# Four stacks of a rounded part and a rest in layers 0 and 1: put together by transfers instead of matrix products

## The reference

```python
# a0: causal windows of 128, 16 heads of 8 features
scores = einsum('bhqd,bhkd->bhqk', wq, wk) * scale
attn = softmax(where(mask, neg, scores));  outs.append(einsum('bhqk,bhkd->bhqd', attn, wv))
# a1: linear attention, 16 heads of 8 features, 64 random features each
q = (x @ Wq).reshape(b, l, 16, 8);  k, v = ...
qf = relu(q @ Wf + bf);  kf = relu(k @ Wf + bf)
kv = einsum('blhf,blhd->bhfd', kf, v)
out = einsum('blhf,bhfd->blhd', qf, kv) / maximum(qf . kf.sum(1), 1e-6)
return out.reshape(b, l, d) @ Wo + bo
```

## Time and profile before

| | us |
|---|---|
| median of 3 runs | 1827.08 (1820.6 to 1829.6) |
| profiled execution, its own time | 1828.14 |
| its span in the trace | 1826.3 |
| PE busy (matrix products) | 1547.0, 85% of the span |
| DVE busy | 1240.9, 68% |
| ACT busy | 1001.1, 55% |
| POOL busy | 792.5, 43% |

### The profile page before, as it was taken

The page is one execution under the profiler, slowest core; times in us unless marked ns, Lnnn a source line. Parts: engine busy times, 40 slices in busy tenths (PEclk is TensorE's granted clock), DMA queues, the critical chain, the costliest instruction groups (busy, mean ns, idle before and its releaser), DMA issues.

```text
span 1826.3 us, 28809 instructions
## 1 busy us (share of the span) xinstructions
PE 1547.0 (85%) x10698; PEld 843.6 (46%) x10748; DVE 1240.9 (68%) x2857; ACT 1001.1 (55%) x1927; POOL 792.5 (43%) x734
## 2 busy tenths in 40 slices
PE   7789889877988898977798888997679898999867
PEld 4555564313555566432355555542135554655214
DVE  5555648998564465799865455499976445559996
ACT  4465436665556443766555544566545654455754
POOL 2231215786133212679614131178941412118892
PEclk9899999978999998988799999999879999989979
DMA  6014302020201430212110152031111015202110
GB/s 234 35 35 129 101 6 76 30 93 17 77 1 35 135 94 7 76 41 81 47 46 1 36 162 73 7 93 45 55 47 41 1 41 167 63 6 93 48 52 12
DMA packets 78028, 111.31 MB, mean 61 GB/s; under 512 B 6208, under 2 KB 56384, under 8 KB 77632
## 3 DMA queue, kind: packets, MB, share of 16 engines
q1 hardware_dynamic: 75840, 105.28, 18.5%
q0 software_dynamic: 2048, 4.20, 0.7%
HBM read 93.73 MB, written 15.73 MB: 60 GB/s over the span
## 4 chain that ended last, share of the span: by engine, by line
PE 47%; DVE 24%; ACT 11%; issue 8%; POOL 6%; DMA 3%; SPq 2%; DVEq 0%; POOLq 0%; ACTq 0%
PE P L241 10%; DVE M L2071 9%; PE P L1685 4%; POOL M L2141 3%; PE P L1914 3%; PE P L409 2%; PE P L2199 2%; PE P L223 2%; DVE st L188 1%; PE P L1861 1%; DVE M L203 1%; PE P L397 1%; ACT P L2006 1%; PE P L981 1%; DVE M L1782 1%
## 5 line engine op out<-in xcount | busy, mean ns | idle before, releaser
L2071 DVE TENSOR_TENSOR_SCAN M<-P,M 128x512 f32<-128x512 f32 x384 | 442.6, 1200 | 22.5 <-ACT P L2006 21.9
L2006 ACT ACTIVATE P<-M,negA 128x512 f32<-128x512 f32 x384 | 262.8, 689 | 175.9 <-DVE M L2071 171.8
L241 PEld LDWEIGHTS P<-wt,M 128*128 128x128 f32 x2176 | 278.8, 196 | 104.6 <-issue 38.7
L241 PE MATMUL P<-wt,M 128*128 128x128 f32 x2176 | 298.0, 284 | 17.5 <-DVE M L1782 6.4
L1914 PE MATMUL P<-M,wt 32*32 32x512 f32 x3072 | 236.0, 689 | 85.2 <-DVE M L2071 62.0
L2141 POOL TENSOR_TENSOR M<-M 128x512 f32<-128x512 f32 x192 | 238.2, 1276 | 96.0 <-ACT M L1988 77.2
L2141 POOL TENSOR_TENSOR M<-W,M 128x512 f32<-128x512 f32 x192 | 244.3, 1306 | 40.9 <-PE P L1914 40.4
L1914 PEld LDWEIGHTS P<-M,wt 32*32 32x32 f32 x3072 | 39.7, 110 | 230.3 <-DVE M L2071 152.9
L1685 PE MATMUL P<-M,wt 128*128 128x512 f32 x256 | 135.8, 612 | 8.0 <-ACT M L1743 4.7
L1782 DVE TENSOR_TENSOR M<-M,P 128x512 f32<-128x512 f32 x128 | 85.8, 675 | 65.5 <-PE P L1693 47.9
L1734 ACT ACTIVATE M<-P 128x512 f32<-128x512 f32 x128 | 75.9, 593 | 90.4 <-PE P L1685 90.1
(11 more groups left out here) (359 smaller groups left out, 3019.9 us busy)
## 6 DMA issues: line engine op xcount, KB each, us to landing
M<-in_e SPq DMA_DIRECT2D x112, 192.0 KB, 2.5
W<-in_e SPq DMA_DIRECT2D x8, 1536.0 KB, 8.0
M<-dt SPq DMA_DIRECT2D x48, 256.0 KB, 4.6
W<-du SPq DMA_DIRECT2D x32, 256.0 KB, 4.9
M<-in_e SPq DMA_DIRECT2D x8, 960.0 KB, 5.3
M<-in_e SPq DMA_DIRECT2D x8, 576.0 KB, 6.4
M<-xs SPq DMA_DIRECT2D x16, 256.0 KB, 3.0
ys<-M SPq DMA_DIRECT2D x16, 256.0 KB, 2.3
```

Of the source, the lines that this page charges most:

```text
L241: m = e.matmul(out[:, tok(j)], h[:, tok(j)], wgt, start=first and j == 0, stop=last, skip_group_check=True)
L2006: e.activation(t["aa"][n % 2][:, :], t["dtr"][i][:, :], EXP, scale=negA[:, c:c + 1]).then_inc(ACT.s, ACT.mark(b, "a3", "aa", n))
L2071: e.tensor_tensor_scan(bb[:, :], t["aa"][n % 2][:, :], bb[:, :], 0.0, MUL, ADD).then_inc(DVE.s, DVE.mark(b, "a3", "scan", n))
```

## The change

1. The selection matrix `sst`, PE's 192 products with it (32 + 32 + 64 + 64) and ACT's 96 copies are gone.
2. A helper `stack_parts` issues three transfers per stack, each of 32 rows by 512 values (64 KB), from the on-chip tiles `hi`, `lo` and `hi` into the stack. All are issued by SP: 12 per item in a0, 24 in a1, 288 in all. Each stack has a semaphore of its own, and PE waits for 48 on it.
3. In a0 the steps stand in `sp_attn0` behind `fetch_firsts`; a1 has a new SP function `sp_attn1`. In a1 stacks of keys and of queries share four tiles (`stk`): the transfer of query stack `g` waits for the key product `kf 2g+1`, the last that reads key stack `g`.
4. In a1 the query projection moves to the front, beside those of keys and values (L903 of the changed kernel; L991 before, after `kv 5`), and the rest of the queries gets a tile of its own.
5. The masks of rows in `by_query` and `by_key` are cut to the 96 and 112 rows that count.
6. All five tables of turns are new.

```diff
+        def stack_parts(e, dst, hi, lo, g, done):
+            r = slice(32 * g, 32 * g + 32)
+            for i, src in enumerate((hi, lo, hi)):
+                e.dma_start(dst.bitcast(f32)[32 * i:32 * i + 32, :], src.bitcast(f32)[r, :]).then_inc(done, 16)
...
         def pe_attn0(e, w, b):
-            def stack_q(g):
-                e.matmul(P[2 + g % 2][:, :], sst[:, tok(g)], qhi[:, :], start=True, stop=False, skip_group_check=True)
-                e.matmul(P[2 + g % 2][0:96, :], sst[:, 128 * g + 32:128 * g + 128], qlo[:, :], start=False,
-                         stop=True, skip_group_check=True).then_inc(PE.s, PE.mark(b, "a0", "stk", g))
...
-                w.wait_ge(DVE.s, DVE.of(b, "a0", "qlo" if g == 0 else "v"))
-                stack_q(g)
             for n, (a, gs) in enumerate(A0_QUERY):
-                if n in (1, 2):
-                    yield
-                    w.wait_ge(ACT.s, ACT.of(b, "a0", "qst", n - 1))
-                    stack_q(n + 1)
                 yield
-                w.wait_ge(ACT.s, ACT.of(b, "a0", "qst", gs[-1]))
+                for g in gs:
+                    w.wait_ge(a0_qst_in[b % 2][g], 48 * (b // 2 + 1))
...
         def act_attn0(e, w, b):
-            for g in range(4):
-                yield
-                w.wait_ge(PE.s, PE.of(b, "a0", "stk", g))
-                e.activation(qst[g][:, :], P[2 + g % 2][:, :], COPY).then_inc(ACT.s, ACT.mark(b, "a0", "qst", g))
...
         def pe_attn1(e, w, b):
-            def stack(hi, g, i, name):
-                a1_bank_free(w, b, i)
-                out = a1_bank(L, i)[0:96, :]
-                e.matmul(out, sst[:, 128 * g:128 * g + 96], hi[:, :], start=True, stop=False)
-                e.matmul(out, sst[:, 128 * g + 32:128 * g + 128], lo[:, :], start=False, stop=True).then_inc(
-                    PE.s, PE.mark(b, "a1", name, g))
             def features(u):
-                w.wait_ge(ACT.s, ACT.of(b, "a1", "kst", g))
+                w.wait_ge(a1_kst_in[b % 2][g], 48 * (b // 2 + 1))
             def qfeat(c):
-                w.wait_ge(ACT.s, ACT.of(b, "a1", "qst", g))
+                w.wait_ge(a1_qst_in[b % 2][g], 48 * (b // 2 + 1))
...
+            e.matmul(a1_bank(L, A1_Q)[:, :], wv("a1q"), xn[:, :], start=True, stop=True).then_inc(
+                PE.s, PE.mark(b, "a1", "q"))
...
         def act_attn1(e, w, b):
-            def copy_stack(dst, g, i, name):
-                w.wait_ge(PE.s, PE.of(b, "a1", name, g))
-                e.activation(dst[0:96, :], a1_bank(L, i)[0:96, :], COPY).then_inc(ACT.s, ACT.mark(b, "a1", name, g))
...
+        def sp_attn1(e, w, b):
+            L, s = lanes[b % 2], b % 2
+            khi, stk, klo, qhi, qlo = L.R[10], L.R[11:15], L.R[15], L.R[16], L.R[6]
+            yield
+            w.wait_ge(POOL.s, POOL.of(b, "a1", "ones"))
+            w.wait_ge(ACT.s, ACT.of(b, "a1", "khi"))
+            w.wait_ge(DVE.s, DVE.of(b, "a1", "klo"))
+            for g in range(4):
+                stack_parts(e, stk[g], khi, klo, g, a1_kst_in[s][g])
+            for g in range(4):
+                yield
+                if g == 0:
+                    w.wait_ge(ACT.s, ACT.of(b, "a1", "qhi"))
+                    w.wait_ge(DVE.s, DVE.of(b, "a1", "qlo"))
+                w.wait_ge(PE.s, PE.of(b, "a1", "kf", 2 * g + 1))
+                stack_parts(e, stk[g], qhi, qlo, g, a1_qst_in[s][g])
...
         def sp_attn0(e, w, b):
             fetch_firsts(e, b, lanes[b % 2].W[:, :], 0, 8)
+            L, va, negm, kst, qst, pT = a0_tiles(b)
+            yield
+            w.wait_ge(ACT.s, ACT.of(b, "a0", "qhi"))
+            w.wait_ge(DVE.s, DVE.of(b, "a0", "qlo"))
+            for g in range(4):
+                stack_parts(e, qst[g], L.R[11], L.R[12], g, a0_qst_in[b % 2][g])
             if 3 <= b + 1 < NB:
...
         TURNS = {
-            "tensor": (2131,
+            "tensor": (2027,
```

More of the change, by code:

```diff
@@ L443, in pe_attn0 @@
                 if n in (6, 7):
-                    w.wait_ge(ACT.s, ACT.of(b, "a0", "qst", n - 4))
+                    w.wait_ge(DVE.s, DVE.of(b, "a0", "v"))
                 elif n > 1:
@@ L899, in a1_bank_free @@
             last = A1_USES[i - 2]
-            if last in ("klo", "qlo"):
-                w.wait_ge(DVE.s, DVE.of(b, "a1", last))
+            if i < 4:
+                w.wait_ge(DVE.s, DVE.of(b, "a1", *last))
             else:
@@ L954, in pe_attn1 @@
             m.then_inc(PE.s, PE.mark(b, "a1", "v"))
-            yield
-            w.wait_ge(DVE.s, DVE.of(b, "a1", "klo"))
-            stack(khi, 0, A1_S[0], "kst")
-            yield
-            stack(khi, 1, A1_S[1], "kst")
+            e.matmul(a1_bank(L, A1_Q)[:, :], wv("a1q"), xn[:, :], start=True, stop=True).then_inc(
+                PE.s, PE.mark(b, "a1", "q"))
             yield
@@ L987, in pe_attn1 @@
                     yield from turn_kv(0)
-                if u == 5:
-                    yield
-                    a1_bank_free(w, b, A1_Q)
-                    e.matmul(a1_bank(L, A1_Q)[:, :], wv("a1q"), xn[:, :], start=True, stop=True).then_inc(
-                        PE.s, PE.mark(b, "a1", "q"))
-                if u >= 6:
-                    yield
-                    w.wait_ge(DVE.s, DVE.of(b, "a1", "qlo"))
-                    stack(qhi, u - 6, A1_QS[u - 6], "qst")
             yield from qfeat(0)
@@ L1104, in dve_attn1 @@
             kvm = L.M[:, 17 * T:17 * T + 256].rearrange("p (c n) -> p c n", c=8)
-            khi, lo, qhi = R[10], R[15], R[16]
+            khi, klo, qhi, qlo = R[10], R[15], R[16], R[6]
             if b == 0:
@@ L1110, in dve_attn1 @@
             w.wait_ge(ACT.s, ACT.of(b, "a1", "khi"))
[L1111 to L1112 removed]
+            e.scalar_tensor_tensor(klo[:, :], a1_bank(L, A1_K)[:, :], 1.0, khi.bitcast(f32), MUL, SUB).then_inc(
                 DVE.s, DVE.mark(b, "a1", "klo"))
             yield
+            w.wait_ge(ACT.s, ACT.of(b, "a1", "qhi"))
+            e.scalar_tensor_tensor(qlo[:, :], a1_bank(L, A1_Q)[:, :], 1.0, qhi.bitcast(f32), MUL, SUB).then_inc(
+                DVE.s, DVE.mark(b, "a1", "qlo"))
+            yield
+            w.wait_ge(POOL.s, POOL.of(b, "a1", "ones"))
             w.wait_ge(PE.s, PE.of(b, "a1", "v"))
@@ L1126, in keys_by_values @@
                                 over_tokens(wv("kvmask")), MUL).then_inc(DVE.s, DVE.mark(b, "a1", "kvm", h))
-            for u in range(8):
-                if u == 5:
-                    yield
-                    w.wait_ge(ACT.s, ACT.of(b, "a1", "qhi"))
-                    w.wait_ge(PE.s, PE.of(b, "a1", "kst", 3))
-                    e.scalar_tensor_tensor(lo[:, :], a1_bank(L, A1_Q)[:, :], 1.0, qhi.bitcast(f32), MUL, SUB).then_inc(
-                        DVE.s, DVE.mark(b, "a1", "qlo"))
-                if u == 4:
-                    yield from keys_by_values(0)
+            yield from keys_by_values(0)
             yield from keys_by_values(1)
```

140 lines of the change are left out of this document (40 added, 100 removed).

## The result

The changed kernel takes 1894.45 us (median of 4 runs, 1885.41 to 1898.59), against 1827.51 for the kernel before in the same session (4 runs, 1820.6 to 1829.6). The ratio is 1.0377, with a 95% interval of 1.0342 to 1.0413. It is slower, by 67 us; I had said 1827, and 1803 to 1846 as the range.

A forecast was written before the change was run, and what follows sets the result against it. The prediction took the touched stages as close to bound by PE, with 10 to 15% idle. From 1828.14 us, +26.5 for the start, −34 for stacks and +6 for waits gave 1826.6, said as 1827, range 1803 to 1846.

The forecast's parts named there:

- Start, +26.5: First pair's a0: first stack lands at 48.0 us behind all first loads, costing 26.5 us with the clock loss.
- three us at half speed: Behind the long wait at the start: the clock falls to 1.2 GHz for three us, losing 1.5 us.
- Stacks, −34: a0 and a1: removing PE's stack products and ACT's copies gains 34 us, between 30.5 and 49.
- What is on the path: Chain from 99.38 to 1512.98 us: stack products 25.1 us and ACT's copies 5.4, together 30.5 us as the gain's lower end.
- my sum: Whole kernel: start, stacks and waits add to 1826.6 us, said as 1827, own range 1817 to 1837; chance 40%.
- Waits, +6: Entries to a0 and a1 behind the start: four of 14 waits for stacks left uncovered at 1.5 us, 6 us.
- the slower rival: a0 and a1 entries: uncovered waits of 17 to 21 us take the gain, 1841 us; chance 23%.
- 0 for the rest: All else, such as DVE, POOL, cut rows, ACT's relief beyond the 5.4 us counted, SP in f1: no effect.
- SP in f1: f1: six stack issues by SP delay the sorted tokens, at most 2 us per pair, 8 in all, 1835 us; chance 6%.
- the cases: Whole kernel: the sum 1827 us (40%), waits 1841 (23%), PE bound 1806 (24%), start not lost 1819 (7%), SP 1835 (6%).

The follow-up runs named there:

- a_start: The changed kernel with the first stacks' transfers issued between the loads of the weights, not behind all loads; 1865.71 us, 1.0234.
- c_old_start: The changed kernel with the turns of the kernel before, and the first stacks' transfers between the loads of the weights; 1875.78 us, 1.0268.
- i_none: The changed kernel in the turns of before, with neither stack transfers nor stack products; readers of a stack read the rounded part; 1850.26 us, 1.0145.
- e_both: c_old_start with the removed stack products issued again beside the transfers, read by nobody; 1861.12 us, 1.0201.
- p_prod: i_none with the removed stack products issued again, read by nobody, and no transfers; 1836.36 us, 1.0070.
- n_new_none: a_start (new turns) with neither stack transfers nor stack products; readers of a stack read the rounded part; 1838.67 us, 1.0069.
- m_new_both: a_start (new turns) with the removed stack products issued again beside the transfers, read by nobody; 1867.31 us, 1.0223.
- k_a1q: The kernel before with transfers for a1's query stacks alone, and the early query projection; 1835.93 us, 1.0067.

## Why the prediction was wrong

**The account.** Span = PE's work at full clock + what the lower clock adds (half of the time at it) + PE's idle time. That half is an upper bound, since PE is idle in part of that time and since products took 1.4 to 1.6 times as long in the rows above, not twice. It is also what the Trainium skill gives as the penalty (TensorE: Matmul & The Clock Gate, "Terms"). From each profile's span, busy time and mean clock, in us:

| kernel | work | clock | idle | span |
|---|---|---|---|---|
| before | 1421 | 126 | 279 | 1826.3 |
| a_start | 1361 | 179 | 325 | 1864.5 |
| c_old_start | 1365 | 184 | 327 | 1875.6 |
| i_none | 1368 | 163 | 317 | 1847.3 |
| e_both | 1417 | 139 | 301 | 1856.7 |
| p_prod | 1424 | 130 | 280 | 1834.0 |

In a_start the change takes 60 us of work away, adds 53 by the clock and 46 of idle time: +38. The differences between the rows are what counts here, not their heights.

**Start, +26.5: right as a sum, with a piece too small.** The wait of 28.03 us, the landing and the row were as said, and a_start measures 24 to 29. But I had three us at half speed, for a loss of 1.5, and it was nearly 12. The first pair ends 35 us late in all, and part of that is not the place in SP's row: a_start still has 16.5 of it.

**Stacks, −34: the step that failed.** The work did go: 0.5 us a stack gave 48, and the account has 56 (1421 to 1365). What failed is "What is on the path": I took each piece on the chain as time that its removal returns. Its removal cost 14 us instead (p_prod to i_none; 15 from e_both to c_old_start). In the score phase DVE sets the pace, and PE's stack products stood in waits that are there anyway. Taking them away made the waits longer, and at 0.50 clock the products left took over the time. c_old_start, e_both, i_none and p_prod show it in the turns of before. In the new turns n_new_none, with neither products nor transfers, is 14 us over the kernel before where my sum had a gain. But m_new_both, with the products back, gains nothing, so the way by waits and clock is there carried over and not shown. I had the earlier trace rows with a wait of 3.53 us and the clock at 0.50 behind it, and priced that once, at the start, with 1.5 us; the same price could fall due wherever the change opens a wait. With neither products nor transfers the kernel was to be 30 to 49 us faster by my sum, and is 24 slower (14 in the new turns). p_prod has PE's products in place and no transfers, and stands 11 us over before. That belongs to what else the new form has, perhaps the early projection (k_a1q has it too, and stands at +12); no run parts them.

**Waits, +6: mis-sized.** The transfers cost 25 to 29 us beside the place in SP's row. In the traces a part of that lies in the first pair (8 of 28 from i_none to c_old_start, 18 of 33 from n_new_none to a_start), and 15 to 20 behind it, against the 6 of my sum. PE's waits ended by a transfer came to 17 us behind the start in the changed kernel, as in the slower rival, for issues of 0.6 to 0.7 us instead of 0.33 and an entry of 4.2 instead of 3.1. Such waits are again no price by themselves: they are 28.6 us in c_old_start, which has only 11 us more idle time than i_none but 21 more by the clock.

**"0 for the rest"**: the new turns were worth −7 to −10, if that is told from chance, SP in f1 about 1 us in the pair read; no run has ACT's relief alone. The range failed as all the cases rested on the stacks' removal being a gain; none had PE's remaining work get slower behind the start.

By terms, each by its distance from the kernel before in its own session, the 67 us are 24 for the start (a_start), 29 for the transfers (n_new_none) and 14 for a kernel with less work and no stack to wait for. None of 15 versions beats the kernel before.

**Open**: why m_new_both gains nothing where e_both gains 15; how the transfers' cost splits between issue, landing and SP's row, and how much of it in a_start and c_old_start is the weights and W0, which now come later (W0 is issued at 52.48 in a_start, 34.92 in the changed kernel); what the early query projection costs.

## What to carry over

Busy time of the bounding engine is not its price: ask whether each removed piece stood in a wait that another engine sets. On TensorE such pieces can also hold the clock, so that removing them costs more than it returns, as in the turns of before here. Before forecasting a gain, look for waits near the place that the change will lengthen, and give the stretch behind them at half speed a case of its own in the range. The test is cheap: put the removed products back, unread, beside the new form, and take both away.

## What was not expected of the hardware

A wait of 1.53 us, with PE busy 0.47 of the 2 us around it, was followed by some 10 us at 1.2 GHz; one of 0.59 us at the same place was not, and neither were waits of 1.51 and 1.66 us elsewhere in the kernel before. At the lower clock the 512-column scores took 0.78 us instead of 0.48 and the mask 0.33 instead of 0.23, less than twice. Transfers of 64 KB over 32 partitions were issued at 0.6 to 0.7 us each in a row (12 in 8.19 us, 14 in 9.94, and 12 in 7.60 in a_start, at 16.61) against 0.33 for one of another kind alone, with 2.0 us to landing in the median over all 288.
